# Layer norms of a post-norm transformer stack: applied by ScalarE in place of VectorE, with mean times factor made by GpSimd

## What is computed

```python
def _layernorm(x, axis=-1, eps=1e-05):
    m = jnp.mean(x, axis=axis, keepdims=True)
    v = jnp.var(x, axis=axis, keepdims=True)
    return (x - m) / jnp.sqrt(v + eps)
```

## Time and profile before

| what | value |
| --- | --- |
| median of 3 runs | 2606.64 us (2605.87 to 2607.78) |
| the profiled execution | 2609.21 us, of which the trace's span is 2607.5 us |
| PE busy | 2398.2 us, 92% |
| DVE busy | 1423.5 us, 55% |
| ACT busy | 1019.9 us, 39% |
| POOL busy | 631.8 us, 24% |
| share of the chain that ended last | PE 60%, issue 26%, DVE 5%, ACT 3%, POOL 3%, DMA 2% |

### The profile page before, as it was taken

One profiled execution on the slowest core, in us unless ns is written; L12 is line 12 of the kernel. 1 busy time (PEld: TensorE's weight loads), 2 busy tenths in 40 slices (PEclk: granted clock), 3 DMA queues, 4 the chain that ended last, 5 costly groups with the idle time before them and its releaser, 6 DMA issues.

```text
span 2607.5 us, 35515 instructions
## 1 busy us (share of the span) xinstructions
PE 2398.2 (92%) x12748; PEld 1262.1 (48%) x12752; DVE 1423.5 (55%) x3163; ACT 1019.9 (39%) x1955; POOL 631.8 (24%) x722
## 2 busy tenths in 40 slices
PE   4576689999999999999999999999987999999998
PEld 3454344555545455455555555555543444444443
DVE  5655578775757667577777777776851110111111
ACT  2455245554444545345545545464651010011000
POOL 4862222332322313123232323232220000000000
PEclk7688889999999999999999999999998999999999
DMA  5000302220310203112121213231203000010000
GB/s 165 1 1 1 106 18 93 95 91 26 97 48 26 93 24 109 54 48 74 65 80 39 87 35 108 74 109 45 88 26 138 0 16 0 0 48 0 16 0 16
DMA packets 90178, 140.82 MB, mean 54 GB/s; under 512 B 8464, under 2 KB 63760, under 8 KB 89232
## 3 DMA queue, kind: packets, MB, share of 16 engines
q1 hardware_dynamic: 90016, 138.71, 16.2%
HBM read 81.93 MB, written 52.56 MB: 52 GB/s over the span
## 4 chain that ended last, share of the span: by engine, by line
PE 60%; issue 26%; DVE 5%; ACT 3%; POOL 3%; DMA 2%; SPq 0%; POOLq 0%; DVEq 0%; ACTq 0%
PE ps L1359 9%; PE ps L1319 8%; PE ps L1301 8%; PE ps L1279 7%; PE ps L1338 6%; PE ps L1196 5%; PE ps L1374 4%; PE ps L1276 3%; PE ps L1406 2%; PE ps L1383 2%; DVE negmax L2034 1%; PE ps L1231 1%; POOL x L1734 1%; ACT big L1583 1%; ACT big L1523 1%
## 5 line engine op out<-in xcount | busy, mean ns | idle before, releaser
L1583 ACT ACTIVATE big<-ps 128x512 f32<-128x512 f32 (+1 forms) x1056 | 570.3, 560 | 631.5 <-PE ps L1301 607.9
L2034 DVE TENSOR_REDUCE negmax<-ps 128x1 f32<-128x512 f32 (+3 forms) x1056 | 647.0, 636 | 298.8 <-PE ps L1279 294.8
L1791 POOL TENSOR_SCALAR_AFFINE_SELECT big<-big 128x512 f32<-128x512 f32 x384 | 256.3, 671 | 974.7 <-ACT big L1583 974.1
L1175 PE MATMUL ps<-xt,big 128*128 128x512 f32 x896 | 391.1, 599 | 3.4 <-ACT xt L1482 3.4
L1301 PE MATMUL ps<-big 99*128 99x512 bf16 (+3 forms) x1536 | 373.5, 304 | 15.4 <-DVE rest L2158 8.0
L1279 PE MATMUL ps<-big 96*128 96x128 bf16 (+3 forms) x1536 | 380.5, 302 | 0.0
L1359 PE MATMUL ps<-big,xt 128*128 128x512 f32 (+1 forms) x768 | 290.7, 487 | 1.1 <-ACT xt L1604 1.1
L1175 PEld LDWEIGHTS ps<-xt,big 128*128 128x128 f32 x896 | 172.1, 193 | 220.4 <-issue 220.4
L1276 PE MATMUL ps<-cbf 128*128 128x128 bf16 (+2 forms) x1056 | 259.8, 246 | 18.4 <-DMA big<-scr_q 12.4
L1319 PE MATMUL ps<-big,vs 128*32 128x512 f32 (+3 forms) x3072 | 250.6, 445 | 2.3 <-POOL big L1791 2.2
L1279 PEld LDWEIGHTS ps<-big 96*128 96x128 bf16 x1536 | 143.1, 98 | 204.0 <-issue 164.5
(11 more groups left out here) (209 smaller groups left out, 2682.7 us busy)
## 6 DMA issues: line engine op xcount, KB each, us to landing
big<-scr_q SPq DMA_DIRECT2D x96, 384.0 KB, 4.0
scr_q<-big SPq DMA_DIRECT2D x48, 384.0 KB, 2.5
scr_q<-big SPq DMA_DIRECT2D x48, 256.0 KB, 2.9
big<-scr_k SPq DMA_DIRECT2D x48, 192.0 KB, 3.5
big<-in_ffn_gu SPq DMA_DIRECT2D x14, 512.0 KB, 8.0
scr_q<-big SPq DMA_DIRECT2D x48, 128.0 KB, 2.7
big<-in_attn_w SPq DMA_DIRECT2D x3, 1536.0 KB, 6.5
scr_k<-big SPq DMA_DIRECT2D x12, 384.0 KB, 2.5
```

Source lines behind the costliest of these rows:

```text
L1175: mm = pe.matmul(ps[:, 2 * (m % 2) + k, :], w(c, m), xt[:, c, :], start=(c == 0), stop=(c == DC - 1))
L1583: act.activation(probs_of(i), bank_of("exp", g, i)[:, 0:len(heads) * w], ACT.Exp, scale=1.0 / 16 if attn_of(n) == 1 else 0.25).then_inc(ma ...
L1791: pool.affine_select(block_, block_, [[0, GQ], [1, P]], ALU.is_ge, zero, base=0, channel_multiplier=-1).then_inc(made["cut"], 1)
L2034: dve.tensor_reduce(negmax[:, p % 2, q, h0:h0 + n], bank_of("max", p, u)[:, 0:n * w].rearrange("p (h k) -> p h k", h=n), AX.X, ALU.max, ne ...
```

## The change

The norms `d` and `f` are made as those of `l` and `q`: the four `tensor_scalar` on DVE go, ACT applies them with four ACTIVATE Identity, and POOL adds the product of negated mean and factor. The planner's durations and needs are changed to match, and so its order may change on every engine. The first 30 lines of the diff drop the helper `normed` and replace its uses and the name `xn` by `nx`; the waits on `xn` in SP and PE become waits on `nx` in the same places.

```diff
     if kind == "ln":
-        return [("DVE", "stats", k, 1250), ("POOL", "rstd", k, 2200 if k[0] in "lq" else 1050)]
+        return [("DVE", "stats", k, 1250), ("POOL", "rstd", k, 2200)]
     if kind == "lnx":
-        return [("ACT", "nx", k, 2600) if k[0] in "lq" else ("DVE", "xn", k, 2800)]
+        return [("ACT", "nx", k, 2600)]
...
             for b in range(NB):
-                wait_made(sp, "xn", "d", 2 * NB + b)
+                wait_made(sp, "nx", "d", 2 * NB + b)
                 load_x(st, b)
...
                 if tag == "f":
-                    wait_made(pe, "xn", "d", n)
+                    wait_made(pe, "nx", "d", n)
                 elif attn_of(n) == 1:
                     wait_made(pe, "nx", "q", n)
                 else:
-                    wait_made(pe, "xn", "f", n - NB)
+                    wait_made(pe, "nx", "f", n - NB)
...
             flow_products()
-            wait_made(pe, "xn", "d", NIT - 1)
+            wait_made(pe, "nx", "d", NIT - 1)
...
                 wait_made(pool, "stats", tag, n)
-                if tag in "df":
-                    pool.tensor_tensor(rstd[:, way], var[:, way], half[:], ALU.pow).then_inc(made["rstd"], 1)
-                    return
                 pool.tensor_tensor(rstd[:, way], var[:, way], half[:], ALU.pow).then_inc(pool_links, 1)
...
                 if j == 0 and nth >= 2:
-                    wait_made(dve, normed(*flow.norms[nth - 2]), *flow.norms[nth - 2])
+                    wait_made(dve, "nx", *flow.norms[nth - 2])
...
-                dve.tensor_scalar(mean, mean, 0.5 if tag in "df" else -0.5, None, ALU.mult)
+                dve.tensor_scalar(mean, mean, -0.5, None, ALU.mult)
...
-            def flow_norm(tag, n):
-                way = flow.norms.index((tag, n)) % 2
-                wait_made(dve, "rstd", tag, n)
-                for j in range(TJ):
-                    last = dve.tensor_scalar(x_rows(n, j), x_rows(n, j), mv[:, way, 2, j:j + 1], rstd[:, way, j:j + 1],
-                                             ALU.subtract, ALU.mult)
-                last.then_inc(made["xn"], 1)
...
-                    elif kind == "xn":
-                        flow_norm(*k)
```

More of the change, by code:

```diff
@@ L201, in experts_work @@
     return items + [(0, ("ln", "f", n)), (0.5, ("gap",)), (0, ("lnx", "f", n))]
-def normed(tag, n):
-    return "nx" if tag in "lq" else "xn"
 LOOK = 40
@@ L417, in order_of @@
         return [("stats", k)]
-    if name in ("xn", "nx"):
+    if name == "nx":
         return [("rstd", k)]
@@ L425, in order_of @@
         if tag == "f":
-            return [("xn", ("d", n))]
-        return [("xn", ("f", n - NB)) if n >= NB else ("nx", ("q", n))]
+            return [("nx", ("d", n))]
+        return [("nx", ("f", n - NB) if n >= NB else ("q", n))]
     if name == "proj":
@@ L648, in needs @@
                 if nth >= 2:
-                    out.append((normed(*self.norms[nth - 2]), self.norms[nth - 2]))
+                    out.append(("nx", self.norms[nth - 2]))
             elif name == "hi":
```

## The result

| | before | changed |
|---|---|---|
| median of 5 runs | 2606.82 us (2605.87 to 2610.91) | **2626.34 us** (2622.92 to 2634.06) |
| ratio, 95% interval | | **1.0076** (1.006 to 1.0093) |
| profiled execution, its span | 2609.21, 2607.5 us | 2622.92, 2621.2 us |

The change costs some 19.5 us. The forecast was 2606.6 and the range ended at 2619. The page of the changed kernel: busy time by engine.

The account below looks back on a forecast made before the run. PE was taken as the bound, with DVE the busiest helper. The terms 0 - 3.0 + 2.0 + 0 + 1.0 + 0 summed to 0, so 2606.6 us for the median; range 2595 to 2619 us.

Parts of the forecast that it names:

- Removed and added instructions: 80 `tensor_scalar` leave DVE, 80 ACTIVATE and 20 POOL products come; DVE down some 48 us, ACT up some 60.
- POOL, 0: Cuts behind POOL's power start up to 0.27 us later; ends 0 and +2.7 us for ten norms, taken as 0.
- The norm of n = 10, +1.0 us: At the end, without PE side work, ACT's 2.93 us are 1.4 too long; ends -0.7 and +1.4, taken as +1.0 us.
- The way into `ffn3`, 0: The n = 11 norm ends 1.14 us before ACT's squares of `ffn3`, so nothing is lost or gained.
- DVE's side of the `d` norms, -3.0 us: Norms of n = 0 to 9: selects come 0.30 us sooner each; ends 0 and 10.7 us gained, taken as -3.0.
- Rival A: DVE is the real bound in the ten `d` norm stretches; its relief gives 2595.2 us; chance 0.30.
- The eight `f` norms: 0: ACT's 2.93 us lie beside PE's projections, with 4.94 us free on ACT; 0, or up to 2.93 us each without cover.
- The step that failed: The planner's new order over 1480 us was given no row, held inside the same ends of -11.4 and +16.3 us.
- ACT's side of the `d` norms, +2.0 us: Norms of n = 0 to 9: ACT some 0.2 us short each; ends 0 and 1.22 us each, taken as +2.0 for ten.
- Rival B: ACT's block delays exponentials, cuts and values in the ten `d` stretches, PE's list being fixed; 2620.2 us, chance 0.25.
- The sign that was named for B: PE's waits for exponentials, 3.8 us before, several times as long, and PE idle ahead of L1319, released by the cuts.
- The sign named for being wrong in kind: Time between two `d` norms changes where PE has side work, or the way into `ffn3` waits for the last norm.

Follow-up runs that it names:

- `pool_only`: Kernel before, norms still on DVE, with POOL also making the product for `d` and `f`, its result unread; 2609.16 us, ratio 1.0.
- `no_norm`: Kernel before with its own lists, `d` and `f` norms not applied, one small DVE instruction in their place; 2610.88 us, ratio 1.0008.
- `new_list_no_norm`: Changed kernel with its lists, `d` and `f` norms not applied, one small ACTIVATE in their place; 2626.77 us, ratio 1.0065.
- `old_order`: Norms on ACT where the changed kernel has them, but PE, DVE, POOL and SP keep the order of the kernel before; 2689.56 us, ratio 1.0309.
- `both_late`: Changed kernel replanned: ACT's `f` norms behind the copies of turned rows, `d` norms behind their group's last exponentials; 2600.11 us, ratio 0.9966.
- `new_list_dve`: Changed kernel's plan, but `d` and `f` norms applied by DVE at the places of the kernel before; 2672.39 us, ratio 1.024.
- `late_list_dve`: Plan with late norm places, but `d` and `f` norms applied by DVE at the places of the kernel before; 2656.06 us, ratio 1.0178.
- `old_late`: Other engines' order from the kernel before, ACT's norms behind copies of turned rows (`f`) or the group's last exponentials (`d`); 2645.44 us, ratio 1.0144.
- `changed_again`: The changed kernel measured once more, nothing altered; 2626.79 us, ratio 1.0072.

## Why the prediction was wrong, point by point

- **What bounds the kernel**: right. PE does, and its waits for `rest` and for ACT (7.0 and 3.8 us) are nearly the same after the change (7.0 and 3.7).
- **Removed and added instructions**: right in kind. 112 ACTIVATE at 802 ns, a block of 2.92 us, products of 0.20, L2103 gone, and the selects beside the place of the norm take 1.22 us a pair, as forecast for DVE's absence. Off in the totals: DVE's busy time fell by 37.1 us and not by some 48 (two of the steps of `split` on 128x32, which now run beside selects, took 6.5 us more in all), ACT's grew by 49.5 and not by some 60. Nor did PE stay above 98% in every stretch: from 700 to 800 us it has 97.17 of 100, before 98.78.
- **POOL, 0**: right with the old lists (`pool_only`).
- **The norm of n = 10, +1.0 us**: nothing was lost there; d9 to d10 took 0.40 us less than before and d10 to d11 0.08 less.
- **The way into `ffn3`, 0**: right, but closer than written. The block ended at 1990.87 and the squares began at 1991.34; the slack was 0.47 us, not 1.14.
- **DVE's side of the `d` norms, -3.0 us**: too large, the value is 0 with the old lists (`no_norm`). The selects come sooner, but nobody was waiting for them; PE's loss stood ahead of the norm, as the text itself said. Rival A falls with it.
- **"The eight `f` norms: 0. The 2.93 us lie beside PE's projections"**: wrong by 1.40 us each, 11 in all. The free time of ACT was counted (4.94 of 12 us) and not whether the projections stay where they were. They went 2.8 us later.
- **The step that failed** is the last one of the sum: "I hold it inside the same ends, because where PE has side work its list is full in any order, and only the ten stretches and the end can move." The planner gave a norm 2600 ns on ACT and pulled scores forward around each of the first sixteen. A list can be full of units and not of work: three scores for maxima in a row stood 0.6 to 0.7 us apart, at the pace of DVE's reductions. `new_list_no_norm` shows the whole price, 17.5 us, with no block at all: this term, put at nothing, is the 17 to 19 us.
- **ACT's side of the `d` norms, +2.0 us**: 0.2 us each was far too small for the block in an unchanged list (3.9 to 5.0 us a d to f interval in `old_order`, the lower clock included), and so was the upper end, which let PE's values cover 1.71 of it. In `old_order` the wait behind the block is 2.38 us alone. With the changed list it is not this term that is paid.
- **Rival B** was nearest in its number (2620.2 us) and on the right side, but by a mechanism that the changed kernel doesn't have: "PE's list is fixed, so it can't step aside". It did step aside, at a smaller price than the block's. The sign that was named for B, PE's waits for exponentials several times as long, is absent after the change and present in `old_order`. The Trainium skill (ScalarE: Activation LUTs, Rules for kernel authors) would keep multiplications and additions off ScalarE. The durations agree with it (1.92 against 2.93 us for a norm), but the outcome depends on the place: `both_late` breaks the rule and is the fastest kernel of this study.
- **The range**: it was said to reach to both rivals, but it ended at 2619 us, below rival B's own 2620.2 and below what the ends of the sum give, 2606.6 + 16.3 = 2622.9. The measured 2626.34 lies outside all three.
- The sign named for being wrong in kind came true: "the time between two `d` norms changed where PE has side work".

What stays open is how the 1.24 us of a `d` norm split. PE's waits for DVE in the waits view are 2.5 us in 11 by scores for maxima (L1272) and 1.8 in 10 by scores for exponentials (L1297, for the division L2057), some 0.4 us a norm; the rest is in gaps and in matmul time, and no run took it apart. Nor was it shown why attention 3 gains 4.7 us with the late places, or how much of the losses of `new_list_dve` and `late_list_dve` (+63 and +47 us) the lower clock makes in all.

## What to carry to other kernels

Where a planner makes the order, a changed cost or place can be a new list for every engine: compare the lists before the durations, and look for runs of units that are short on the bound engine and long on its helper. Here moving a block off a helper paid only with the new owner having it at a place where nothing behind it was due, and with the plan made for that place: place and plan together gave -7.8 us, late places with the old lists +37, the plan with the norms on DVE +47, the last two with a part that came with a lower clock. To tell block from list, keep the list and shrink the block. To tell waits from clock, compare equal intervals with the granted clock beside them.

## What the runs showed that was not expected

- PE's busy time isn't a count of work. From the `d` norm of n = 2 to the next `f` norm the same matmuls (408 and 407) took 75.43 us before and 75.99 after; from d8 to d9 the same 796 took 111.69 and, in `both_late`, 110.02. One f32 product, which is two records, takes 1.10 us alone (L1359 at 952.42 in the kernel before), and six records, three products, take 2.74 (L1355 at 955.17 in the changed kernel), so in a row each further product adds some 0.8: whatever breaks a row adds busy time too. Idle time by itself shows 0.64 of 1.20 us in the first case. That all of the rest comes from broken rows was not shown.
- Ahead of ten norms, the `d` norms of n = 0 to 9, DVE's first small operation of the statistics takes 1.03 to 1.10 us; ahead of the other `d` and the `f` norms it takes 0.15 to 0.17. The long one starts beside a sum of POOL of 1.15 us, and both end together (changed kernel, n = 2):

```profile
868.87 1.15 POOL L1776 TENSOR_TENSOR big<-rest,big 128x512 bf16<-128x512 f32 x1 [3.28 <-ACT big L1627]
869.00 1.04 DVE L2084 TENSOR_TENSOR mv<-stat 128x4 f32<-128x4 f32 x1
...
869.97 0.15 DVE L2085 TENSOR_TENSOR mv<-stat 128x4 f32<-128x4 f32 x1
```

  So it stands on the way to the power of these ten, before and after alike. That POOL's sum holds it is argued from the common end; it was not tried to move it.
- Executions of one kernel differ by several us ahead of the first `d` norm (its power at 556.60 us in one profile of the changed kernel and 562.9 in the other), and by less than 0.05 us in nearly every interval behind it. Intervals between landmarks told differences apart that the medians, uncertain by 2 to 4 us either way, could not.
- Four kernels of this study with long waits of PE (`old_order`, `old_late`, `new_list_dve`, `late_list_dve`) had stretches at the 1.2 GHz level between the first and the last `d` norm; the kernel before, `changed_again` and `both_late` had none, and the changed kernel's first profile had one, of 3.4 us.
